# Chunks 3 to 6 of u transposed outside TensorE, in a one-core Griffin and MLP kernel

## What is computed

```python
t   = rmsnorm(x, norm1_w)
xb  = causal_conv4(t @ Wx) + conv_b
r,i = sigmoid(xb @ Wa), sigmoid(xb @ Wi)
a   = exp(-8 * softplus(lam) * r)
h   = scan over tokens of h = a*h + sqrt(max(1 - a*a, 1e-12)) * (i*xb)
h1  = x + (h * gelu(t @ Wy)) @ Wo
u   = rmsnorm(h1, norm2_w)
x1  = layernorm(x + h1 + (gelu(u @ Wg) * (u @ Wu)) @ Wd)
out = layernorm(x1 + relu(x1 @ W1 + b1) @ W2 + b2)
```

## Time and profile before

| what | value |
|---|---|
| median of 3 runs | 587.02 us (586.99 to 587.03) |
| the profiled execution's own time | 587.02 us |
| its span (first to last instruction) | 585.2 us, so 1.8 us lie around it |
| TensorE busy | 578.5 us (99%) |
| VectorE, ScalarE, GpSimd busy | 401.0 (69%), 314.6 (54%), 203.8 (35%) us |
| TensorE's share of the chain that ended last | 97% |
| granted TensorE clock | 0.998 of full, so the upper level, 2.4 GHz |

### The profile page before, as it was taken

How to read it: one execution, slowest core, us unless ns; L and a number is a source line. 1 busy time by engine, 2 the same in 40 slices (tenths; PEclk the granted TensorE clock), 3 DMA queues, 4 the chain that set the end, 5 groups by cost and what they waited for, 6 DMA issues and landing times.

```text
span 585.2 us, 9307 instructions
## 1 busy us (share of the span) xinstructions
PE 578.5 (99%) x3441; PEld 511.9 (87%) x3441; DVE 401.0 (69%) x729; ACT 314.6 (54%) x600; POOL 203.8 (35%) x282
## 2 busy tenths in 40 slices
PE   8999999999999999999999999999999999999996
PEld 8768988898888988898888888889888898888996
DVE  5888958867739668495765848568595765563565
ACT  7977675834548444573446634575343843232454
POOL 2111336273233542255233452424523233140130
PEclk9999999999999999999999999999999999999999
DMA  7400210011100121001210031100200010101011
GB/s 275 149 36 25 84 36 2 2 29 44 37 0 1 27 84 36 1 1 38 73 37 0 1 82 38 26 2 8 65 22 16 1 34 5 34 3 37 1 38 36
DMA packets 27197, 21.46 MB, mean 37 GB/s; under 512 B 3448, under 2 KB 26384, under 8 KB 27152
## 3 DMA queue, kind: packets, MB, share of 16 engines
q1 hardware_dynamic: 27152, 20.87, 11.8%
HBM read 10.89 MB, written 4.19 MB: 26 GB/s over the span
## 4 chain that ended last, share of the span: by engine, by line
PE 97%; DVE 1%; POOL 0%; issue 0%; ACT 0%; DVEq 0%; POOLq 0%; ACTq 0%
PE psum L454 18%; PE psum L456 18%; PE psum L455 18%; PE psum L465 11%; PE psum L467 11%; PE psum L466 11%; PE psum L545 2%; PE psum L472 1%; PE psum L838 1%; PE psum L510 1%; PE psum L676 1%; PE psum L678 1%; PE psum L674 1%; PE psum L572 1%; PE psum L529 1%; PE psum L489 0%
## 5 line engine op out<-in xcount | busy, mean ns | idle before, releaser
L1903 POOL TENSOR_SCALAR gu_hi<-gu_raw 128x512 fp32r<-128x512 f32 x64 | 54.4, 851 | 262.0 <-DVE gu_raw L1514 262.0
L1092 ACT ACTIVATE hid_raw<-psum,vecs 128x512 f32<-128x512 f32 x56 | 38.4, 686 | 115.4 <-PE psum L456 115.3
L1514 DVE TENSOR_TENSOR gu_raw<-psum,gu_raw 128x512 f32<-128x512 f32 x64 | 44.0, 687 | 69.9 <-PE psum L456 69.9
L1524 DVE TENSOR_TENSOR hid_lo<-hid_raw,hid_hi 128x512 fp32r<-128x512 f32 x56 | 40.7, 728 | 47.2 <-ACT hid_hi L1096 47.2
L465 PE MATMUL psum<-w_d_hi,gu_hi 128*128 128x256 f32 x256 | 72.2, 282 | 0.0
L465 PE MATMUL psum<-w_hi,hid_hi 128*128 128x256 f32 x256 | 71.9, 281 | 0.2 <-DVE hid_lo L1524 0.2
L467 PE MATMUL psum<-w_d_hi,gu_lo 128*128 128x256 f32 x256 | 71.8, 281 | 0.0
L467 PE MATMUL psum<-w_hi,hid_lo 128*128 128x256 f32 x256 | 71.8, 281 | 0.0
L466 PE MATMUL psum<-w_lo,hid_hi 128*128 128x256 f32 x256 | 71.7, 280 | 0.0
L466 PE MATMUL psum<-w_d_lo,gu_hi 128*128 128x256 f32 x256 | 71.7, 280 | 0.0
L1077 ACT ACTIVATE gu_raw<-psum 128x512 f32<-128x512 f32 x64 | 38.1, 595 | 50.3 <-PE psum L456 49.7
(11 more groups left out here) (237 smaller groups left out, 1530.7 us busy)
## 6 DMA issues: line engine op xcount, KB each, us to landing
out_dram<-row SPq DMA_DIRECT2D x15, 256.0 KB, 2.4
xs<-in_L_attn_x_dram SPq DMA_DIRECT2D x7, 512.0 KB, 3.7
gy<-normed SPq DMA_DIRECT2D x96, 32.0 KB, 1.9
t_raw<-t_blocks SPq DMA_DIRECT2D x80, 32.0 KB, 1.9
raw_gud<-in_L_attn_Wg_dram SPq DMA_DIRECT2D x1, 1024.0 KB, 8.1
raw_gud<-in_L_attn_Wu_dram SPq DMA_DIRECT2D x1, 1024.0 KB, 10.2
raw_gud<-in_L_attn_Wd_dram SPq DMA_DIRECT2D x1, 1024.0 KB, 12.4
raw_gud<-in_L_ffn_W_dram SPq DMA_DIRECT2D x1, 1024.0 KB, 6.6
```

Of the source, the lines that this page charges most:

```text
L1092: nc.scalar.activation(raw, hidden, ACT.Relu, bias=vec("b1", m)).then_inc(relu_ready, 1)
L1514: nc.vector.tensor_tensor(gu_raw[:, r % SLOTS, :], up_bank(r)[:, :], gu_raw[:, r % SLOTS, :], ALU.mult).then_inc(gu_ready, 1)
L1524: nc.vector.tensor_tensor(hid_lo[:, w % SLOTS, :], hid_raw[:, w % SLOTS, :], hid_hi[:, w % SLOTS, :].bitcast(FP32), ALU.subtract).then_inc ...
L1903: nc.gpsimd.tensor_scalar(gu_hi[:, r % SLOTS, :], gu_raw[:, r % SLOTS, :], 1.0, 0.0, ALU.mult, ALU.add).then_inc(gu_hi_ready, 1)
```

## The change

u of chunks 3 to 6 is transposed as t is: `transpose_u_blocks` on VectorE in round m=6, then 12 DMAs for the blocks off the diagonal (8 from SyncE, 4 from ScalarE's queue) and 4 copies on GpSimd for the blocks on the diagonal. The four diagonal blocks of t go to GpSimd too. mix_y, the scan and gelu(y) stand a round sooner, and so do t's split and mix_x. u of chunk 7 is still transposed by TensorE, with its splits behind the relus. The matmuls are the same in number but for the transposes.

```diff
+        OFF_DIAGONAL = [(i, j) for i, j in ALL_BLOCKS if i != j]
+        ACT_MOVES = 4
...
 # SyncE
             def move_t(c):
                 sync.wait_ge(t_blocks_ready, KD * (c - BLOCKWISE + 1))
-                move_blocks(flat(t_blocks), flat(t_raw), t_blocks_moved)
+                for i, j in OFF_DIAGONAL:
+                    move_block(sync, flat(t_blocks), flat(t_raw), t_blocks_moved, i, j)
...
+            def move_u(c):
+                sync.wait_ge(u_blocks_ready, KD * (c - BLOCKWISE + 1))
+                for i, j in OFF_DIAGONAL[ACT_MOVES:]:
+                    move_block(sync, flat(u_blocks), flat(u_raw), u_blocks_moved, i, j)
...
                 if c >= BLOCKWISE:
                     move_t(c)
                 if c >= 4:
+                    move_u(c - 1)
                     store_out(c - 4)
...
 # TensorE
                 if m == 0:
-                    pe.wait_ge(uT_lo_ready, 2 * c + 2)
+                    pe.wait_ge(uT_lo_ready, 2 * c + (1 if c >= BLOCKWISE else 2))
...
+                for k in range(KD):
+                    if m == 0 and k == KD - 1:
+                        pe.wait_ge(uT_lo_ready, 2 * c + 2)
+                    last = product_step(gate_bank(r)[:, :], "g", m, k, uT_hi, uT_lo)
...
                     up(r)
+                if mixing and m == 4 and p >= 2:
+                    mix_y(n)
+                if n == LAST and m == 7:
+                    transpose_u(n)
                 if mixing and m == 3 and p >= 1:
                     mix_decay(n)
-                if mixing and m == 7 and p >= 2:
-                    transpose_u(n)
...
-                if mixing and m == 0 and p >= 2:
+                if r == 2 * KH:
                     mix_x(n)
-                if mixing and m == 4 and p >= 1:
+                if m == 7 and p >= 2 and n + 1 < CHUNKS:
+                    mix_x(n + 1)
+                if r == KH + 4:
                     mix_y(n)
...
 # ScalarE
+            def move_u(c):
+                act.wait_ge(u_blocks_ready, KD * (c - BLOCKWISE + 1))
+                for i, j in OFF_DIAGONAL[:ACT_MOVES]:
+                    move_block(act, flat(u_blocks), flat(u_raw), u_blocks_moved, i, j)
...
+                if m == 7 and p >= 2 and n < LAST:
+                    move_u(n)
                 if units(r):
                     gelu_gate(r)
                 if mixing:
-                    if m == 0 and p >= 2:
+                    if m == 7 and p >= 2 and n < LAST:
+                        split_t_hi(n + 1)
+                    if r == 2 * KH:
                         split_t_hi(n)
...
                         square_decay(n)
+                        if p >= 2:
+                            gate_scale(n)
...
-                if mixing:
-                    if m == 7 and p >= 2:
-                        split_hi(uT_hi, uT_done, uT_hi_ready, n)
                 for w in second_units(r):
                     relu(w)
...
                     if m == 0:
                         conv_start(n, 0)
+                        if p >= 3:
+                            conv_start(n, 1)
+                    if m == 7 and p >= 2:
+                        if n < LAST:
+                            split_u_hi(n)
+                        else:
+                            split_last_u_hi()
                     if m == 4:
-                        gate_scale(n)
+                        if p == 1:
+                            gate_scale(n)
                         act.preload_act_table(ACT.Gelu_apprx_tanh)
+                        if p >= 2:
+                            gelu_y(n)
...
 # VectorE
+                if m == 6 and second:
+                    statistics(s, 1, 0, s2_ready)
+                    statistics(s, 1, 1, s2_ready)
+                if m == 5 and mixing and p >= 2:
+                    hy_lo(n)
                 if units(r):
                     gate_times_up(r)
+                if m == 5 and p >= 2 and n < LAST:
+                    transpose_blocks(n + 1)
+                if m == 6 and p >= 2 and n < LAST:
+                    transpose_u_blocks(n)
+                if m == 7 and p >= 2 and n < LAST:
+                    split_t_lo(n + 1)
...
                 if units(r):
                     gate_lo(r)
...
-                if m == 6 and second:
+                if m == 7 and second:
                     normalise(s, 1, 0, out_ready)
                     normalise(s, 1, 1, out_ready)
...
                     if m == 4:
                         room(n)
+                        if p >= 2:
+                            scan_both(n)
+                            gated(n)
...
                 for w in second_units(r):
                     hidden_lo(w)
+                    if m == 7 and mixing and p >= 2:
+                        split_u_lo(n)
...
 # GpSimd
+            def place_u_diagonal(c):
+                pool.wait_ge(u_blocks_ready, KD * (c - BLOCKWISE + 1))
+                for i in range(GROUPS):
+                    nc.gpsimd.tensor_copy(blocks_at(flat(u_raw), i, i),
+                                          blocks_at(flat(u_blocks), i, i)).then_inc(u_diagonal_placed, 1)
+                    pool.wait_ge(u_diagonal_placed, GROUPS * (c - BLOCKWISE) + i + 1)
...
-                if p == 1 and m == 7:
+                if mixing and m == (7 if p == 1 else 6):
                     norm_u(n)
                 if r < UNITS:
                     gate_hi(r)
+                if (r == FROM or m == 5 and p >= 2) and n < LAST:
+                    place_t_diagonal(n + 1)
+                if m == 6 and p >= 2 and n < LAST:
+                    place_u_diagonal(n)
...
+                if m == 4 and p >= 2 and n + 1 < CHUNKS:
+                    norm_t(n + 1)
+                if m == 6 and second:
                     for q in range(PAIRS):
                         ln_scale(s, 1, q)
```

More of the change, by code:

```diff
@@ L66, in griffin_mlp_kernel @@
         tT_lo = sb("tT_lo", [P, KD, T], FP32R)
+        with nc.sbuf_tensor("u_blocks", [P, KD, T], FP32) as u_blocks, nc.sbuf_tensor("u_raw", [P, KD, T], FP32) as u_raw:
+            pass
         mT_hi = sb("mT_hi", [P, KD, T], FP32R)
@@ L224, in by_token, with blocks_at, move_block @@
             return ap.rearrange("p (t i s) -> p t i s", i=GROUPS, t=TT)
-        MOVES = GROUPS * GROUPS * DMA
+        def blocks_at(ap, rows, cols):
+            return ap.rearrange("p (k g a) -> p k g a", k=KD, g=GROUPS)[rows * BLOCK:(rows + 1) * BLOCK, :, cols, :]
+        def move_block(queue, src, dst, moved, i, j):
+            queue.dma_start(blocks_at(dst, j, i), blocks_at(src, i, j)).then_inc(moved, DMA)
+        ALL_BLOCKS = [(i, j) for i in range(GROUPS) for j in range(GROUPS)]
+        OFF_DIAGONAL = [(i, j) for i, j in ALL_BLOCKS if i != j]
+        ACT_MOVES = 4
+        MOVES = len(ALL_BLOCKS) * DMA
+        OFF_MOVES = len(OFF_DIAGONAL) * DMA
         def by_blocks(c):
@@ L633, in gate @@
                     split_done("g")
-                product(gate_bank(r)[:, :], "g", m, uT_hi, uT_lo).then_inc(gate_done, 1)
+                for k in range(KD):
+                    if m == 0 and k == KD - 1:
+                        pe.wait_ge(uT_lo_ready, 2 * c + 2)
+                    last = product_step(gate_bank(r)[:, :], "g", m, k, uT_hi, uT_lo)
+                last.then_inc(gate_done, 1)
             def up(r):
@@ L1175, in round_of @@
                 mixing = n < CHUNKS
-                if mixing and m == 1:
+                if r == 2 * KH + 1 or r == KH + 1:
                     conv_start(n, 1)
@@ L1307, in transpose_blocks, with transpose_u_blocks, split_u_lo @@
                                         ).then_inc(t_blocks_ready, 1)
-            def transpose_x1_blocks(c):
-                dve.wait_ge(uT_done, 2 * (c + 2))
+            def transpose_u_blocks(c):
+                dve.wait_ge(u_ready, u_tiles(c))
+                for k in range(KD):
+                    nc.vector.transpose(u_blocks[:, k, :].rearrange("p (j t s) -> p t j s", j=GROUPS, t=TT),
+                                        normed[:, :, k * P:(k + 1) * P].rearrange("p t (j s) -> p t j s", j=GROUPS)
+                                        ).then_inc(u_blocks_ready, 1)
+            def split_u_lo(c):
+                for f in range(KD):
+                    dve.wait_ge(uT_hi_ready, 2 * c + f + 1)
+                    transposes = u_raw[:, f, :] if c < LAST else psum[MIX + f][:, :]
+                    nc.vector.tensor_tensor(uT_lo[:, f, :], transposes, uT_hi[:, f, :].bitcast(FP32),
+                                            ALU.subtract).then_inc(uT_lo_ready, 1)
+            def transpose_x1_blocks(c):
+                if c + 1 < BLOCKWISE:
+                    dve.wait_ge(uT_done, 2 * (c + 2))
+                elif c + 1 == LAST:
+                    dve.wait_ge(uT_done, 2 * BLOCKWISE + 2)
+                else:
+                    dve.wait_ge(u_blocks_ready, KD * (c + 2 - BLOCKWISE))
                 dve.wait_ge(x1_ready, TT * c + TT)
@@ L1640, in round_of @@
                     second_sum(s)
```

(13 more changed lines are left out.)

66 lines of the change are left out of this document (44 added, 22 removed).

## The result

The changed kernel takes 593.6 us, the median of four runs (591.87 to 593.96), against 587.02 (586.99 to 587.15) of the kernel before: a ratio of 1.0106, with a 95% interval of 1.0086 to 1.0125. The forecast was 590.7, slower, with a range up to 593.8. The sign is right and the size 2.9 us too small. The profiled execution took 593.62 us, its span 591.8.

The account below looks back on a forecast made before the run. TensorE, busy 99% of the span, was taken as the bound; -3.5 (transposes) + 4.8 (chunks 3 to 6) + 1.3 (chunk 7) + 1.0 (first copies) = +3.6, taken as 3.7 on 587.0: 590.7 us, range up to 593.8.

Parts of the forecast that it names:

- What bounds the kernel: Whole kernel: TensorE is busy 99% of the span without a gap, so every gap the change makes is paid in full.
- The removed transposes, -3.5: TensorE, chunks 3 to 6: four groups of transposes at 0.87 us each leave the chain, 3.5 us saved.
- The wait of chunks 3 to 5, 1.2 each: First gates of chunks 3 to 6: TensorE waits 1.2 us a chunk for uT_lo, bounds 0.4 to 1.9.
- I take 277.1: GpSimd in round m=7: assumed end of two ln_scale, between 276.5 and up to 1.3 us later, before gu_hi at 277.7.
- normalise, 1.38 us: VectorE in round m=7: normalise, moved from m=6, takes 1.38 us between gate_lo and hidden_lo, before uT_lo's first half.
- normalise holds GpSimd up too: Rival for round m=7: normalise takes turns with add_x_h1, 1.3 us more a chunk, 595.9 us; chance 0.04.
- Chunk 6, 1.2: First gate of chunk 6: the same 1.2 us wait for uT_lo as at each of chunks 3 to 6.
- the issues are slow: Rival: ScalarE's four DMA issues take 1.2 us each, delaying gelu; 2.5 us a chunk, 595.9 us; chance 0.10.
- Chunk 7, 1.3: First gate of chunk 7: uT_lo, split behind ScalarE's relus, comes 1.3 us late, bounds 1.1 to 1.5.
- The first copies of t, 1.0: GpSimd at chunk 3: diagonal copies ahead of add_b2 make hidden_lo late and cost 1.0 us, bounds 0 to 1.3.
- What was costed at nothing: Moved work claimed hidden at no cost: mix_y, gate_scale, gelu_y, scan, hy_lo, statistics, norm_t, conv_start and mix_x.
- the wakes: Semaphore wakes over the whole kernel: the sum of +3.6 us was taken as 3.7 for them.

Follow-up runs that it names:

- the kernel with four moves: Changed kernel with normalise behind the splits (not last period), chunk 7's split early, t's first copies late, add_x_h1 of chunks 3 to 6 a round later: 585.81 us.

## Why the prediction was right in sign and 2.9 us short

- **What bounds the kernel: right.** TensorE had no slack, and each gap was paid in full: the distances of the gates account for the whole difference.
- **The removed transposes, -3.5: right.** In the kernel with four moves they give 0.91 us a chunk, against 0.87.
- **The wait of chunks 3 to 5, 1.2 each: right in size, by two errors that cancel.** The first gates wait 1.14, 1.06 and 1.11 us, 1.38 to 1.41 with the slow start behind the wait. u_blocks came at 271.07 on the prediction's clock (271.0 forecast), the gelu's end at 274.6 (274.5), the first half of uT_lo at 282.1 (282.2). Between them two steps failed. gu_hi ended at 276.4, not 277.7. The copies ended at 273.6, not 274.4: each took 0.62 us instead of 0.55, but the four ran through from 271.1 beside gate_lo and hidden_lo, for which the forecast had let them stand 1.2 us. And "I take 277.1" for ln_scale had 0.6 us of a collision in it that did not come. The other way, "normalise, 1.38 us" was too short: 2.36. VectorE was free at the same moment, by another way.
- **The rival "normalise holds GpSimd up too" was true**, and my argument against it was not sound. I compared 1.3 ns a column with 0.7 and took the slower one for a read through one port. But the same rows say that a tensor_scalar of half the columns takes 0.345 us instead of 0.375: as far as two different instructions can be compared, nearly all of it is a fixed cost, and the rate says nothing of ports. The runs with normalise moved (1.37 alone) and add_x_h1 moved (2.68 for two tiles beside it) show the collision. By the Trainium skill (SBUF — State Buffer, Who interferes with whom), float32 tensor_scalar in SBUF can take the pair of ports that VectorE shares with GpSimd, and holds it for the whole instruction. That agrees with these rows, and the tier table that I had set against the row was the better witness. Its price was 1.0 us, not 1.3, since gate_lo had already used up a part of add_x_h1's time: only normalise's first tile was held (1.38 us from 279.60 in the rows above), until add_x_h1 ended at 280.83.
- **Chunk 6, 1.2: short by 0.8.** Its wait is 1.72. Timeline of ScalarE and its queue in the changed kernel before chunk 4 and before chunk 6, with two single issues of chunk 6:

```profile
272.11 2.81 ACTq L236 DMA_DIRECT2D u_raw<-u_blocks  x4
...
275.03 0.60 ACT L1128 ACTIVATE gu_raw<-psum 128x512 f32<-128x512 f32 x1 [2.64 <-issue]
...
413.24 3.46 ACTq L236 DMA_DIRECT2D u_raw<-u_blocks  x4
...
415.15 1.54 SPq L236 DMA_DIRECT2D u_raw<-u_blocks  x1
415.42 1.28 ACTq L236 DMA_DIRECT2D u_raw<-u_blocks  x1
...
416.81 0.60 ACT L1128 ACTIVATE gu_raw<-psum 128x512 f32<-128x512 f32 x1 [3.29 <-issue]
```

  ScalarE's four issues take 2.81 us, 0.70 each (0.64 was taken), but 3.46 at chunk 6, where SyncE's eight take 6.02 instead of 5.07. The gelu comes 0.65 later, and with it everything behind. It is one issue in each queue that is slow, the fourth, and both end at 416.7; the others take 0.6 to 0.9 as elsewhere. So something held both queues to the same moment: it is not the rival "the issues are slow", in which every issue is dearer. The kernel with 6 matmuls in the wait shows what the hold costs. There ScalarE's four issues were over before it,

```profile
413.14 2.82 ACTq L236 DMA_DIRECT2D u_raw<-u_blocks  x4
```

  only SyncE's fifth was held (1.31 us), and chunk 6's round m=7 took 10.90 us instead of 11.53, as those of chunks 3 to 5 (10.88 to 10.95). In every other kernel in which ScalarE issues four, they take 3.3 to 3.8 us at chunk 6. With two they are over in time (1.50), which agrees with the 0.8 us won; what holds the queues there stays open.
- **Chunk 7, 1.3: the term most mis-sized, 3.67.** The forecast's bound was right by itself: with normalise out of the way the wait is 1.3, set by the relus and hidden_lo. But in the changed kernel VectorE was later still. Its timeline there:

```profile
489.09 1.77 DVE L1605 TENSOR_TENSOR gu_lo<-gu_raw,gu_hi 128x512 fp32r<-128x512 f32 x1 [0.74 <-POOL gu_hi L2017]
490.79 2.35 DVE L1564 TENSOR_SCALAR row<-row,ln_mv,ln_rstd 128x256 f32<-128x256 f32 x4
...
493.66 1.28 DVE L1385 TENSOR_TENSOR uT_lo<-psum,uT_hi 128x512 fp32r<-128x512 f32 x2
```

  The prediction had followed only ScalarE for this chunk, though it had just worked out the same queue of gate_lo, normalise and hidden_lo for the others; normalise's 1.38 was in none of its steps here. The wait became 1.76 us, the round 1.92 longer, and the clock's fall, which no rival held, put most of another 1.75 us on top in three of four runs.
- **The first copies of t, 1.0: 0.49**, within its bounds. I had rms 1.4 us late, and it was 0.8 late.
- **What was costed at nothing held**: no wait of TensorE names mix_y, the scan, gelu_y, norm_t, t's moves or the statistics. By the Trainium skill (DMA: Bandwidth & Descriptors, Issuing engines are not separate DMA queues), issuing from several engines saves the sequencer's time. That agrees with 4.0 us lost when SyncE issues all twelve.

The parts in order: -0.5 at the first copies, +0.6 at chunks 3 to 5, +0.8 at chunk 6, +2.4 at chunk 7, -0.3 elsewhere: 3.0 us by these rounded parts, where 2.9 were missing (the forecast had 0.1 for the wakes beside its terms).

That 593.6 still lies within the range up to 593.8 is luck. The upper end was made of waits of 1.9 us at each of chunks 3 to 6; those came near 1.4 three times, and 2.4 of the 2.9 us came at chunk 7, to which the bounds gave 0.2.

## What to carry to other kernels

Where TensorE has no slack, taking work from it pays only if the operands that replace it come in time: here 3.5 us of removed work turned into a loss of 6.6, and into a gain of 3.1 once three steps were put into another order and two DMA issues into another queue, with no further work taken out. Follow every engine of the last step before a wait to its end, for each place where the step occurs, the last one too. When a collision is removed by moving one of its two operations, look at what the operation now stands beside.

## What the runs showed of the hardware that I had not expected

- A tensor_scalar on 256 columns from SBUF stands still beside GpSimd's tensor_tensor of SBUF operands: two tiles 2.68 us instead of 0.7. Its own rate (0.345 us a tile) gives no hint of that.
- TensorE's clock fell to 0.50 after one wait of 1.76 us inside a stretch that is otherwise full, for some 3 us and 1.6 us of time, in five of eight runs; with 6 or 16 matmuls that nobody needs in the wait it fell in none of nine. A wait of 1.72 us elsewhere did not bring it.
- Behind a wait on uT_lo the second matmul starts 0.34 us after the first instead of 0.23, and the round that it opens takes 0.12 to 0.19 us more than one without a wait.
- Four DMA issues in a row held ScalarE for 2.81 us. At one place of the launch a single issue in each of the two queues took 1.28 and 1.54 us instead of 0.6, both ending at the same moment.
- A copy of 32 partitions and 256 columns took GpSimd 0.62 us (2.49 for four), hardly less than the 0.70 of an addition over 128 partitions (2.81 for four).
